# ScalarE's copy of the projection one group later, the last batches' additions and some loads moved, four turns of the prologue as a loop: a state-space block gated by a mixture of experts

## The reference, cut to what matters

```
# s: a Mamba block (256 inner channels, 64 states)
h = layernorm(xn);  x_ssm, z = split(h @ Win)
x_ssm = silu(conv4(x_ssm));  dt = softplus(x_ssm @ dt_w + dt_b)
Bt = x_ssm @ Bp;  Ct = x_ssm @ Cp
state[t] = state[t-1] * exp(dt[t] * A) + (dt[t] * x_ssm[t]) * Bt[t]      # per channel and state
y[t] = sum over the 64 states of state[t] * Ct[t]
s = xn + ((y + x_ssm * D) * silu(z)) @ Wout
# g: silu(xn + 2 shared experts + the best 2 of 8 routed experts, each weighted by its gate)
g = silu(xn + shared(xn) + sum_k gate_k * expert_k(xn))
```

## Time and profile before

| | |
|---|---|
| runs (3) | 2003.87, 2011.78, 2013.79 us, median 2011.78 |
| the profiled execution | 2002.24 us, its span 2000.5 us |
| mean granted TensorE clock | 0.918 of full speed |
| busy | DVE 86%, PE 82%, ACT 68%, POOL 68% |
| first and last scan (L1145) | 275.4 and 1983.9 us |
| costliest groups of instructions | scans (DVE) 1178.6 us, products with C (POOL) 1203.2 us, decays (ACT) 673.5 us, sums of y (PE) 571.5 us |

### The profile page before, as it was taken

One profiled execution on the slowest core, in us unless ns is written; L12 is line 12 of the kernel. 1 busy time (PEld: TensorE's weight loads), 2 busy tenths in 40 slices (PEclk: granted clock), 3 DMA queues, 4 the chain that ended last, 5 costly groups with the idle time before them and its releaser, 6 DMA issues.

```text
span 2000.5 us, 41953 instructions
## 1 busy us (share of the span) xinstructions
PE 1636.5 (82%) x12738; PEld 810.6 (41%) x12738; DVE 1725.3 (86%) x1906; ACT 1367.1 (68%) x2511; POOL 1366.8 (68%) x675
## 2 busy tenths in 40 slices
PE   1771638999899989998999899997877888877887
PEld 1540324444444444444444444442433333433433
DVE  6792638999799979997999899999896889978897
ACT  3571657888588858885788677768675677648672
POOL 5047006777577757775777677778886779867785
PEclk9786769999899999998999999999898899989899
DMA  8342363556555665555545555555446345543443
GB/s 232 122 172 87 109 184 89 134 121 146 125 124 128 149 139 123 121 146 128 131 124 132 141 132 127 129 136 119 101 106 149 78 103 110 125 101 93 107 99 65
DMA packets 202352, 249.45 MB, mean 125 GB/s; under 512 B 26082, under 2 KB 104364, under 8 KB 202092
## 3 DMA queue, kind: packets, MB, share of 16 engines
q1 hardware_dynamic: 198164, 239.78, 49.9%
q0 software_dynamic: 4096, 8.40, 1.3%
HBM read 204.00 MB, written 43.66 MB: 124 GB/s over the span
## 4 chain that ended last, share of the span: by engine, by line
PE 29%; issue 24%; DVE 18%; ACT 9%; POOL 8%; DMA 6%; another core or an unknown queue 3%; SPq 2%; DVEq 1%; ACTq 0%; POOLq 0%
DVE arena L1145 9%; PE ps L1319 9%; POOL arena L657 7%; PE ps L1333 6%; DVE ps L1135 6%; ACT arena L882 4%; DMA arena<-attn_sum_scratch 2%; PE ps L1404 2%; ACT arena L888 2%; PE ps L1305 1%; PE ps L1217 1%; PE ps L1280 1%; PE ps L1380 1%; DMA arena<-c_scratch 1%
## 5 line engine op out<-in xcount | busy, mean ns | idle before, releaser
L657 POOL TENSOR_TENSOR arena<-arena 128x1024 f32<-128x1024 f32 x512 | 1203.2, 2363 | 500.9 <-DVE arena L1145 407.3
L1145 DVE TENSOR_TENSOR_SCAN arena<-arena,ps 128x512 f32<-128x512 f32 x1024 | 1178.6, 1205 | 133.1 <-PE ps L1319 129.2
L882 ACT ACTIVATE arena<-arena,neg_A 128x512 f32<-128x512 f32 (+1 forms) x1024 | 673.5, 716 | 89.4 <-DVE arena L1145 88.5
L1333 PE MATMUL ps<-arena,ident 64*64 64x512 f32 x4096 | 571.5, 630 | 2.9 <-POOL arena L657 2.8
L1319 PE MATMUL ps<-arena 128*64 128x128 f32 x6144 | 443.8, 289 | 126.7 <-DVE arena L1145 120.2
L1319 PEld LDWEIGHTS ps<-arena 128*64 128x64 f32 x6144 | 347.5, 143 | 446.1 <-DVE arena L1145 283.9
L1135 DVE TENSOR_TENSOR ps<-arena,ps 128x512 f32<-128x512 f32 x640 | 406.9, 683 | 35.7 <-PE ps L1305 34.9
L888 ACT ACTIVATE arena<-ident,b_turned 128x128 f32<-128x128 f32 x768 | 243.6, 391 | 0.0
L1333 PEld LDWEIGHTS ps<-arena,ident 64*64 64x64 f32 x4096 | 109.8, 134 | 166.3 <-issue 166.3
L625 POOL DMA_INDIRECT x_rms_by_expert<-arena,slots x64 | 64.7, 1011 | 109.2 <-DVE slots L1097 90.0
L1305 PE MATMUL ps<-b_parts,pick 120*128 120x512 bf16 x320 | 124.3, 388 | 16.2 <-DVE arena L1145 15.9
(11 more groups left out here) (166 smaller groups left out, 1039.6 us busy)
## 6 DMA issues: line engine op xcount, KB each, us to landing
arena<-c_scratch SPq DMA_DIRECT2D x128, 1024.0 KB, 8.6
arena<-w_routed_scaled SPq DMA_DIRECT2D x40, 256.0 KB, 5.9
arena<-in_L_ffn_W_r_dram SPq DMA_DIRECT2D x40, 256.0 KB, 8.5
arena<-w_shared_tiles SPq DMA_DIRECT2D x128, 64.0 KB, 7.3
x_rms_by_expert<-arena SPq DMA_DIRECT2D x1, 5120.0 KB, 23.2
arena<-x_rms_by_expert SPq DMA_DIRECT2D x40, 128.0 KB, 7.2
routed_by_expert<-arena SPq DMA_DIRECT2D x40, 128.0 KB, 8.3
sz_scratch<-arena SPq DMA_DIRECT2D x8, 512.0 KB
```

What stands on the lines that cost most here:

```text
L657: nc.gpsimd.tensor_tensor(products[:, i % RING, :, :], states[:, i % 2, :, :], c_rows[:, i // CG, i % CG, :].unsqueeze(1).broadcast_to((P, ...
L882: nc.scalar.activation(decay[:, 2 * i + h, :], dflat[:, ds(slot + h * L, L)], ACT.Exp, scale=aflat[:, ds(col, 1)]).then_inc(s["decay_ready ...
L1145: vector.tensor_tensor_scan(states[:, i % 2, h, :], decay[:, m, :], ps[bank][:], 0.0, ALU.mult, ALU.add).then_inc(s["scanned"], 1)
L1333: ins = mm(y_ps[r][HP * h:HP * h + HP, :], ident[q, q], products[q, slot, h, :], start=False, stop=False, skip_group_check=True)
```

## The change

Four edits go together.

1. ACT's `evict_attn` leaves the end of the head group and goes into group 1 of the batch, before the decays of its step 5. For that ACT's group 1 is written out, and its inner loop runs over groups 2 to 7.
2. `ADD_IN` becomes 43, 46, 49, 52, 55, 58, 61. `load_final` is issued one group earlier. On PE `begin_final` and the first half of the rows go from step 7 of the group before to step 1 of the group itself, the second half from step 0 to step 2. The last batch's gate diagonals are made in group 62 instead of 61.
3. SP issues the first shared and routed weights ahead of the first loads of C (the wait for the slots comes with them).
4. Turns 3 to 6 of the prologue are a loop of two rounds of two turns on SP, ACT, DVE and PE; turns 1, 2 and 7 stay written out.

```diff
-    gather_group = lambda f: NBLK + (GATHERS * f + GATHERS - 1) // len(GATHER_AT)
-    ADD_IN = [gather_group(f) + 1 for f in range(NB - 1)]
+    ADD_IN = [NBLK + 3 + 3 * f for f in range(NB - 1)]
...
-        turns = [(b, b % 2) for b in range(1, NB)]
+        def turns(engine):
+            yield 1, 1
+            yield 2, 0
+            with engine.Fori(0, (NB - 4) // 2) as pair:
+                yield pair * 2 + 3, 1
+                yield pair * 2 + 4, 0
+            yield NB - 1, 1
...
-                if isinstance(u, int) and u in FINAL_OF:
-                    load_final(FINAL_OF[u])
+                if isinstance(u, int) and u + 1 in FINAL_OF:
+                    load_final(FINAL_OF[u + 1])
...
+            sp.wait_ge(s["slots_made"], 1)
+            e = expert_of(0)
+            load_w1_shared(0, 0)
+            load_w2_shared(0, 0)
+            load_w1_b1(0, e)
+            load_w2(0, e)
             sp.wait_ge(s["dt_u_made"], NB + 1)
             load_c(0, 0, 0)
             load_c(0, 0, 1)
...
             load_open(0)
             load_xn(0)
             load_xn(1)
-            load_w1_shared(0, 0)
-            load_w2_shared(0, 0)
-            sp.wait_ge(s["slots_made"], 1)
-            e = expert_of(0)
-            load_w1_b1(0, e)
-            load_w2(0, e)
             sp.wait_ge(s["x_sorted"], 16 * TOPK * NT)
             load_x_rows(0)
...
-            def group(b, g, slot, head, block, block_before, last=None):
+            def group(b, g, slot, head, block, block_before, last=None, project=None):
...
+                    if i == 5 and project is not None:
+                        evict_attn(project)
...
-                        f = FINAL_OF.get(u, NB - 1 if u == ADD_IN[-1] + 2 else None)
+                        f = FINAL_OF.get(u, NB - 1 if u == ADD_IN[-1] + 1 else None)
...
                 hidden_tiles(u, g, block)
-                if head and last is not None:
-                    evict_attn(last)
...
                 group(b, 0, slot, True, blocks, not first and (blocks or after_blocks), None if first else b - 1)
+                group(b, 1, slot, False, blocks, blocks, project=None if first else b - 1)
                 if blocks:
-                    with act.Fori(1, E) as g:
+                    with act.Fori(2, E) as g:
                         group(b, g, slot, False, True, True)
...
-                        if u + 1 in FINAL_OF and i == SG - 1:
-                            begin_final(FINAL_OF[u + 1])
-                            add_rows(FINAL_OF[u + 1], 0, block_ps)
-                        if u in FINAL_OF and i == 0:
+                        if u in FINAL_OF and i == 1:
+                            begin_final(FINAL_OF[u])
+                            add_rows(FINAL_OF[u], 0, block_ps)
+                        if u in FINAL_OF and i == 2:
                             add_rows(FINAL_OF[u], 1, block_ps)
```

More of the change, by code:

```diff
@@ L368, in _ @@
             store_x(0, 0)
-            for b, odd in turns:
+            for b, odd in turns(sp):
                 store_z(b)
@@ L772, in _ @@
                                 ).then_inc(s["scores_ready"], 1)
-            for b, odd in turns:
+            for b, odd in turns(act):
                 pad(b)
@@ L901, in run @@
                 group(b, 0, slot, True, blocks, not first and (blocks or after_blocks), None if first else b - 1)
+                group(b, 1, slot, False, blocks, blocks, project=None if first else b - 1)
                 if blocks:
-                    with act.Fori(1, E) as g:
+                    with act.Fori(2, E) as g:
                         group(b, g, slot, False, True, True)
                 else:
-                    for g in range(1, E):
+                    for g in range(2, E):
                         group(b, g, slot, False, False, False)
@@ L1099, in _ @@
             choose_experts()
-            for b, odd in turns:
+            for b, odd in turns(dve):
                 convolve(b, b * NL + (base + NCONV - NL))
-                if b == 2:
+                if isinstance(b, int) and b == 2:
                     place_tokens()
@@ L1224, in project_dt_b_c @@
                 pe.wait_ge(s["bt_copied"], b + 1)
-                if b == 1:
+                if isinstance(b, int) and b == 1:
                     pe.wait_ge(s["slots_counted"], 2)
@@ L1238, in _ @@
             pe.wait_ge(s["scores_ready"], 1)
-            for b, odd in turns:
+            for b, odd in turns(pe):
                 project_in(b)
-                if b == 2:
+                if isinstance(b, int) and b == 2:
                     pe.wait_ge(s["slots_projected"], 1)
```

## The result

| | before | after |
|---|---|---|
| median | 2011.04 us (4 runs, 2003.87 to 2013.79) | 1923.82 us (4 runs, 1920.91 to 1926.92) |
| the profiled execution | 2002.24 us, span 2000.5 | 1926.92 us, span 1925.2 |
| granted TensorE clock | 0.918 | 0.935 |

The ratio is 0.9572, 95% interval 0.9543 to 0.9601: 87.2 us less at the median. Traces must therefore be summed against 75.3, not 87.2.

The account below looks back on a forecast made before the run. DVE, busy 86% of the span and held by PE, was taken as the bound. 25.1 + 13.3 + 46.2 + 3.9 - 1.0 = 87.5 us off the profiled 2002.2 gave 1914.7, for the median 1924.3 us; 8-in-10 range 1868 to 1952.

Parts of the forecast that it names:

- Heads of batches 1 to 4: Copying the projection later cuts DVE's waits there from 37.1 us to 3.0 us a head: 25.1 us saved.
- Heads of the last batches and additions: Late gelus after heads 5 to 7 no longer hold PE, 13.3 us; waits at the seven additions mostly go, 46.2 us.
- I give it 1 us of DVE each: Additions' second half, moved to step 2, still costs DVE 1 us at each of seven, 7 us in all.
- the loads are a group (24 us) earlier ... so both waits go: At the additions, PE's waits for stored sums (19.9 us) and for the last gather (13.5 us) both vanish.
- Edit 3: First group: earlier weights free the first fill, but PE next waits for turn_x's rows; 3.9 us saved, bounds -3.4 to 24.4.
- I charge 1 us for the four turns: Prologue loop: one branch back and some register arithmetic per engine cost 1 us in all.
- the wait of the earlier trace as the upper bound: Prologue loop: its cost lies between 0 and one wait like ACT's 29.42 us stand in turn 4.
- the 9.5 us between profile and median: Whole kernel: the profiled execution was 9.5 us below the three runs' median, so 1914.7 became a median of 1924.3 us.
- the additions give half: Rival: step 2 or the later silu costs DVE up to 38 us instead of 7, giving 1949 us; chance 0.12.
- PE is late in the heads by itself: Rival: moving the projection's copy gives only ACT's freedom, 25 us stay in the heads, 1949 us; chance 0.06.
- The prologue's stall goes with the loop: Rival: looping removes ACT's 29.42 us stand in turn 4, up to 50 us more, giving 1874 us; chance 0.14.
- Code has to be fetched behind the scatter: Rival: in the prologue's loop each fetch costs 29.4 us; 1954 us for one; chance 0.05 for one to three, 0.03 beyond.

Follow-up runs that it names:

- edit 4 alone: The kernel before with only turns 3 to 6 of the prologue made a loop: 2020.4 us, ratio 1.0061.
- the halved scatter: The kernel before with GpSimd's scatter cut to one of each token's two experts (32 indirect transfers for 64), output not the reference's: 1978.78 us, ratio 0.9848.

## Why the prediction was right

The time, 1924.3 forecast and 1923.8 measured, is nearer than the working deserves. Point by point:

- **Heads of batches 1 to 4: 25.1 us forecast, 25.8 measured in the waits.** The 3.0 us left of each head were 2.83, with waits near those read off the head of batch 5 (2.01 for 1.75, and 0.82). ScalarE's 14.34 us for the projection are gone. What the working left out is the clock: it put all of the 7.77 and 10.78 us down to the work that queued behind TensorE's stand, and part of them was the same work at a granted clock of 0.50 (16 products of a fill in 1.98 us for 1.09). The size came out all the same, because without the stand the low clock stayed away too.
- **Heads of the last batches and additions: 13.3 + 46.2 = 59.5 us forecast, 65.0 measured.** The reading was right: TensorE's own waits for stored sums and gathered rows had held the scans. The term mis-sized is "I give it 1 us of DVE each" for step 2, 7 us in all: it cost nothing. The step that said "the loads are a group (24 us) earlier ... so both waits go" gave the load a share that it does not have; the place of the addition is enough.
- **Edit 3: 3.9 us forecast, 2.8 in after's batch 0 and 4.3 alone.** What was late next was named rightly: the rows for `turn_x`, still issued behind the same waits. TensorE stood 18.63 us for them. The loads' order saves only what lies between the two.
- **Edit 4: "I charge 1 us for the four turns".** The two traces give 9.1 us in the prologue, the edit alone cost 12 at the median. I had given the wait of the earlier trace rows as the upper bound, and that held. It also won: by the place it gives to ScalarE's loop over batches, it takes the second stand away and makes the ends of batches about 3 us shorter each, 7 to 9 us in all. Taken back from the changed kernel as a whole it gave no gain.
- **ScalarE's longer loop: no term in the sum, -13.3 us in the traces.** That the loops of the kernel before go round without a wait, 23.89 us a group, is true, and it was the wrong question: edit 1 makes the body of one of them longer. Nor do speak of ScalarE. Their q8 is TensorE's queue: in before, from 1400 to 1900, where TensorE's groups are written out, it brings one packet of 16 KB for every 253 of TensorE's instructions. ScalarE's is q14, which moved nothing from 545 to 700. What the runs show in place of a price: 6.78 to 7.28 us without an instruction at the branch, three times, 44 instruction packets for 28, and both the stands and 10 of the packets gone with the loop written out. A loop of 213 instructions went round without a wait, one of 301 did not, at any of the places that it had. ScalarE's packets are of 8 KB (44 packets, 0.36 MB). At which length between 213 and 301 the stand begins, and what sets that length, no run here measured.
- **The offset.** 87.5 us forecast; by the steps above 25.8 + 65.0 + 2.8 - 9.1 - 13.3 = 71.2, with 5 us of small waits that I did not price, makes the 76.1 between the traces. The medians differ by 87.2. The missing 11 us are in which execution was profiled. I added the 9.5 us between profile and median on one side and took it for constant; that the total still came out is luck: the steps were some 11 us too high against the traces, and the traces lie some 12 us closer together than the medians. A part may be the clock in the heads: the ends of batches took 108.5 to 111.4 us in before's trace, 112.7 to 112.9 each in the traces of edit 4 alone and of the halved scatter, whose code for the batches is that of the kernel before. If the unprofiled runs of before had those, they were 10 us longer. Eleven runs of before in the last round agree in kind: they reach from 2000.18 us at a granted clock of 0.922 to 2019.08 at 0.912, while the four runs of after lie within some 6 us. That is argued, not shown.

Of the rivals, "the additions give half" and "PE is late in the heads by itself" were out by the rows above. "The prologue's stall goes with the loop" fell with the loop run alone, and the halved scatter showed what the argument against it had named. "Code has to be fetched behind the scatter" did not come: no run shows a fetch that costs 29.4 us, and the loop's price at the worst was 9 us in the prologue and 12 us in the time of the edit alone. What did come is a stand of 6.8 to 7.9 us at another branch, ScalarE's over batches 1 to 4, for which DVE paid 3 to 6 us each.

## What to carry to other kernels

When an edit writes out one more turn inside a loop, price the body of the loop as well as the work: count its instructions, look for idle time at the branch back, whatever releaser the row names, and at packets of that engine's instruction queue inside it. Where an engine's wait costs more than its length, look at TensorE's granted clock behind it. An edit's cost can sit in the place that it gives to other code of the same engine, so take edits back one at a time from the full set, not only put them in alone; here that turned 12 us of loss into nothing and pointed to 20 us more. And where two changes move an operation and its load, try the operation alone first.

## What the hardware showed that I had not expected

- A branch back on ScalarE over a body of 301 instructions left 6.8 to 7.9 us without an instruction; over 213 its next register operation came 0.25 us later. How much of it DVE lost (3.2 to 6.1 us a batch against the written-out form, 6.1 to 8.1 with the loop further on in the code) depended on where the loop lies, though the wait itself stayed at 7 us: further on in the code a second stand of 1.8 to 2.1 us came behind it, with a packet of the instruction queue inside.
- The same stand of TensorE (3.36 and 3.35 us) was followed by 3.4, 10.2 or 13.7 us at a granted clock of 0.50, and DVE's wait behind it was 4.09, 6.64 or 7.92 us. What sets the length stays open.
- While GpSimd issues 64 indirect transfers (118 to 202 us, one per 1.3 us) one hand-over from TensorE to ScalarE came late: its semaphore moved 33.6 us after the product that sets it, and ScalarE stood 29.42 us (38.60 in after); with 32 transfers the first scan comes 39.9 us earlier. TensorE, ScalarE and DVE share no data with that scatter in these turns. Whether it is the issuing or the transfers that hold it stays open, as does why the first scan's place differs by up to 9 us (274.0 to 283.3) between kernels whose prologue is the same.
